# Third layer's heads: the first products and both turns take turns over three PSUM banks, and value products go two key blocks at a time

## The reference

```python
q, k, v = (split_heads(q), split_heads(k), split_heads(v))
scores = jnp.einsum('bhqd,bhkd->bhqk', q, k) * scale
attn = jnp.einsum('bhqk,bhkd->bhqd', jax.nn.softmax(scores, axis=-1), v)
combined = g * mem_out + (1.0 - g) * attn
```

## Time and profile before

| | us |
|---|---|
| median of 3 runs | 4081.96 (4080.65 to 4087.51) |
| profiled execution, its own time | 4091.38 |
| span of the profiled execution | 4089.6 |
| stage of the heads in it | from about 2301 to 2774 |
| TensorE busy over the span | 3655.6 (89%) |
| VectorE busy over the span | 2325.4 (57%) |
| ScalarE busy over the span | 1598.5 (39%) |
| mean granted TensorE clock | 0.929 of full speed |

### The profile page before, as it was taken

One profiled execution on the slowest core, in us unless ns is written; L12 is line 12 of the kernel. 1 busy time (PEld: TensorE's weight loads), 2 busy tenths in 40 slices (PEclk: granted clock), 3 DMA queues, 4 the chain that ended last, 5 costly groups with the idle time before them and its releaser, 6 DMA issues. The chain is left out here.

```text
span 4089.6 us, 65022 instructions
## 1 busy us (share of the span) xinstructions
PE 3655.6 (89%) x21096; PEld 2662.2 (65%) x21096; DVE 2325.4 (57%) x4783; ACT 1598.5 (39%) x2884; POOL 1389.7 (34%) x1087
## 2 busy tenths in 40 slices
PE   6999999999797999999966799997899979999676
PEld 4777777777575888888833344443678737776354
DVE  3555555555325566666647778774566646666444
ACT  2444444444233444444423166662333333333211
POOL 1333333333135666666614000000223352334254
PEclk8999999999898999999978799998899989999755
DMA  0000000000001000000004122210333313332144
GB/s 35 5 5 5 3 5 5 5 3 5 32 0 45 18 17 20 18 17 17 8 3 183 42 74 76 76 65 26 83 82 87 90 34 76 91 82 54 57 103 95
DMA packets 115990, 178.66 MB, mean 44 GB/s; under 512 B 22288, under 2 KB 65040, under 8 KB 115600
## 3 DMA queue, kind: packets, MB, share of 16 engines
q1 hardware_dynamic: 109776, 169.38, 13.8%
q0 software_dynamic: 6144, 8.39, 1.3%
HBM read 151.51 MB, written 25.95 MB: 43 GB/s over the span
## 5 line engine op out<-in xcount | busy, mean ns | idle before, releaser
L424 POOL TENSOR_TENSOR l0h_probs<-l0h_probs,l0h_inv 128x128 f32<-128x128 f32 (+7 forms) x256 | 292.8, 1146 | 585.7 <-DVE l0h_inv L459 585.7
L1747 DVE TENSOR_REDUCE l2h_half<-l2h_s 128x1 f32<-128x512 f32 x512 | 329.6, 685 | 94.2 <-PE l2h_s L1658 94.1
L1734 ACT ACTIVATE l2h_PT<-l2h_s 128x1024 f32<-128x1024 f32 x256 | 261.9, 1023 | 194.2 <-PE l2h_s L1668 194.2
L355 PE MATMUL l0h_sc<-l0a_KT,l0h_QT 128*128 x768 | 296.7, 499 | 30.0 <-ACT l0h_probs L528 28.3
L382 PE MATMUL l0h_cx<-l0h_PT,l0h_VG 128*128 128x128 f32 x2304 | 300.7, 276 | 0.0
L528 ACT ACTIVATE l0h_probs<-l0h_sc,l0h_negtop 128x128 f32<-128x128 f32 (+7 forms) x256 | 189.6, 741 | 245.4 <-DVE l0h_negtop L454 245.0
L382 PEld LDWEIGHTS l0h_cx<-l0h_PT,l0h_VG 128*128 128x128 f32 x2304 | 278.0, 192 | 1.1
L159 POOL TENSOR_TENSOR XN<-XN,n_rstd 128x512 f32<-128x512 f32 x32 | 39.8, 1265 | 635.2 <-DVE n_rstd L140 635.2
L2189 DVE TENSOR_TENSOR_SCAN l3p_table<-l3p_decb,l3p_eye 128x512 f32<-128x512 f32 x128 | 149.8, 1212 | 116.0 <-DMA l3p_prow<-l_decays 92.2
L1658 PE MATMUL l2h_s<-l2h_K,l2h_Q 128*128 128x512 f32 x512 | 180.2, 429 | 21.7 <-DMA l2h_K<-l_split 18.0
L452 DVE TENSOR_REDUCE l0h_top<-l0h_sc 128x1 f32<-128x128 f32 (+7 forms) x256 | 194.0, 758 | 8.8
(11 more groups left out here) (410 smaller groups left out, 9081.1 us busy)
## 6 DMA issues: line engine op xcount, KB each, us to landing
l3p_decb<-l_decays SPq DMA_DIRECT2D x128, 256.0 KB, 5.2
l3p_w<-L_w SPq DMA_DIRECT2D x34, 512.0 KB, 5.9
l2h_Q<-l_split SPq DMA_DIRECT2D x64, 256.0 KB
l2h_K<-l_split SPq DMA_DIRECT2D x64, 256.0 KB
l3p_prow<-l_decays SPq DMA_DIRECT2D x128, 128.0 KB, 5.6
l_split<-l2q_hi SPq DMA_DIRECT2D x16, 512.0 KB, 4.0
l_split<-l2q_lo SPq DMA_DIRECT2D x16, 512.0 KB, 3.8
mx_wgu<-L_ffn_w_gate_up SPq DMA_DIRECT2D x32, 256.0 KB
```

What stands on the lines that cost most here:

```text
L355: mm = pe.matmul(sc[u % 2][:, lo:lo + n], QT[:, u * P:(u + 1) * P], KT[:, ds(g, 1), b * S + lo:b * S + lo + n], start=True, stop=True)
L424: pool.tensor_tensor(p, p, inv[:, u % 4:u % 4 + 1].to_broadcast([P, keys(u)]), ALU.mult).then_inc(probs_scaled, 1)
L1734: act.activation(PT[:, b, kb, :], s2[kb % 2][:, :], ACT.Exp, scale=L2_SCALE).then_inc(exped, 1)
L1747: dve.reduce_max(half[:, b, t, z:z + 1], s1[i % 2][:, :], AX_X).then_inc(maxed, 1)
```

## The change

The first products get three banks instead of two, and the bank of the turns goes: both turns now use the same pool. Each job has 18 slots in a fixed order: products 0 and 1, the maxima's turn (slot 2), the context's turn (slot 3), products 2 to 15 (slots 4 to 17); slot s uses bank s % 3. One semaphore, `s1_read`, counts every read of a slot in this order: the maximum of a product, the second half of the split, the normalisation. Who writes slot s waits until slot s - 3 is read. `read_up_to` works out the count for a slot; the first jobs lack some turns, which it takes into account. `m_ready`, `maxed` and `ctx_kept` go.

TensorE's order changes too. For two key blocks it was S S F F V, S S F F V (S second product, F first product, V the value products of a block). Now it is F S S F S S, then in the first pair of a job the turn of the maxima and the turn of the context, then F F V V. VectorE reads two products, then splits, normalises, and reads the other fourteen (before: four, then twelve). SyncE waits for the split by `s1_read`.

```diff
-        s1 = [st.ps(f"s1_{i}") for i in range(2)]
+        s1 = [st.ps(f"s1_{i}") for i in range(3)]
-        turns, pv = st.ps("turns"), st.ps("pv")
+        pv = st.ps("pv")
-        TURN_AT = 1
+        TOP_SLOT, CTX_SLOT, SLOTS = 2, 3, NP + 2
+        READ_BY_LAST = SLOTS * (L2_N - 2) + 31
+        def slot_of(i):
+            return i if i < TOP_SLOT else i + 2
+        def bank(slot):
+            return s1[slot % 3]
+        def read_ahead(n):
+            if isinstance(n, int) and n < 2:
+                return {-2: 0, -1: NP, 0: 2 * NP + 1, 1: 3 * NP + 2}[n]
+            return SLOTS * n + 31
+        def read_up_to(n, slot):
+            missing = () if not isinstance(n, int) or n >= 2 else (TOP_SLOT, CTX_SLOT) if n == -2 else (CTX_SLOT,)
+            return read_ahead(n) + slot + 1 - sum(m <= slot for m in missing)
...
-                    sp.wait_ge(m_ready, n + 1)
+                    sp.wait_ge(s1_read, top_read(n))
...
-                        wait(pe, maxed, NP * n + i - 1)
-                        pe.matmul(s1[i % 2][:, :], Q1[:, b, t * P:(t + 1) * P], K1[:, b, z * BANK:(z + 1) * BANK],
+                        wait(pe, s1_read, read_up_to(n - 2, slot_of(i) - 3))
+                        pe.matmul(bank(slot_of(i))[:, :], Q1[:, b, t * P:(t + 1) * P], K1[:, b, z * BANK:(z + 1) * BANK],
...
+                def turn_top(n, of, read):
+                    pe.wait_ge(top_ready, n + 1)
+                    pe.wait_ge(s1_read, read)
+                    pe.transpose(bank(TOP_SLOT)[0:NQ, 0:P], top[:, of, :], k.ident[:, :]).then_inc(top_turned, 1)
+                def turn_ctx(j, read):
+                    pe.wait_ge(pv_kept, j + 1)
+                    pe.wait_ge(s1_read, read)
+                    for i in range(2):
+                        mm = pe.transpose(bank(CTX_SLOT)[:, i * P:(i + 1) * P], ctxT[:, i * P:(i + 1) * P], k.ident[:, :])
+                    mm.then_inc(ctx_turned, 1)
...
                 def step(h, b):
-                    for kb in range(NQ):
-                        second_pass(h, b, kb)
+                    n = B * h + b
+                    for kb in range(0, NQ, 2):
+                        for i in range(2):
+                            if exists(h, b, 2):
+                                first_pass(*after(h, b, 2), (2 * kb + i,))
+                            second_pass(h, b, kb + i)
+                        if kb == 0:
+                            if exists(h, b, 1):
+                                turn_top(n + 1, 1 - b, READ_BY_LAST if not exists(h, b, 2) else read_up_to(n, TOP_SLOT - 3))
+                            if not isinstance(h, int) or h > 0:
+                                turn_ctx(n - 2, READ_BY_LAST + 2 * b if not exists(h, b, 2) else read_up_to(n, CTX_SLOT - 3))
                         if exists(h, b, 2):
-                            first_pass(*after(h, b, 2), range(2 * kb, 2 * kb + 2))
-                        if kb == TURN_AT:
-                            turn(B * h + b + 1, not isinstance(h, int) or h > 0, (b + 1) % B if exists(h, b, 1) else None)
+                            first_pass(*after(h, b, 2), (2 * kb + 2, 2 * kb + 3))
                         if not is_first(h, b):
-                            values(*before(h, b), kb)
+                            for i in range(2):
+                                values(*before(h, b), kb + i)
...
-                    early = 2 * (TURN_AT + 1)
                     if more:
-                        maxima(*after(h, b, 2), range(early))
+                        maxima(*after(h, b, 2), range(TOP_SLOT))
```

More of the change, by code:

```diff
@@ L1552, in l2_heads @@
         VH = st.sb("VH", [P, 2, NQ, L2_W])
-        s1 = [st.ps(f"s1_{i}") for i in range(2)]
+        s1 = [st.ps(f"s1_{i}") for i in range(3)]
         s2 = [st.ps(f"s2_{i}", 2 * BANK) for i in range(2)]
-        turns, pv = st.ps("turns"), st.ps("pv")
+        pv = st.ps("pv")
         ctxT = st.sb("ctxT", [P, 2 * P])
-        pmt = turns[0:NQ, NQ * L2_W:NQ * L2_W + P]
         filled, q1_loaded = st.sem("filled"), [st.sem(f"q1_loaded{i}") for i in range(B)]
         q2_loaded, m_loaded = [st.sem(f"q2_loaded{i}") for i in range(B)], [st.sem(f"m_loaded{i}") for i in range(B)]
-        s1_made, maxed, top_ready = st.sem("s1_made"), st.sem("maxed"), st.sem("top_ready")
-        mhi_ready, m_ready, s2_made, exped = st.sem("mhi_ready"), st.sem("m_ready"), st.sem("s2_made"), st.sem("exped")
-        pv_made, pv_kept, turned, inv_ready, ctx_kept = (st.sem(n) for n in ("pv_made", "pv_kept", "turned", "inv_ready", "ctx_kept"))
+        s1_made, s1_read, top_ready = st.sem("s1_made"), st.sem("s1_read"), st.sem("top_ready")
+        mhi_ready, s2_made, exped = st.sem("mhi_ready"), st.sem("s2_made"), st.sem("exped")
+        pv_made, pv_kept, top_turned, ctx_turned, inv_ready = (st.sem(n) for n in ("pv_made", "pv_kept", "top_turned", "ctx_turned", "inv_ready"))
         vh_ready, second_loads = st.sem("vh_ready"), st.sem("second_loads")
         NP = 2 * NQ
-        TURN_AT = 1
+        TOP_SLOT, CTX_SLOT, SLOTS = 2, 3, NP + 2
+        READ_BY_LAST = SLOTS * (L2_N - 2) + 31
         MROW = SPLIT
@@ L1609, in load_second, with top_read @@
                     load(Q2[:, b, :], K2[:, b, :], h, b, q2_loaded[b])
+                def top_read(n):
+                    return READ_BY_LAST + 1 if isinstance(n, int) and n == L2_N - 1 else read_up_to(n - 1, TOP_SLOT)
                 def load_max(h, b):
                     n = B * h + b
-                    sp.wait_ge(m_ready, n + 1)
+                    sp.wait_ge(s1_read, top_read(n))
                     for i, m in enumerate((mhi, mlo)):
@@ L1683, in values @@
                         mm.then_inc(pv_made, 1)
[L1685 to L1690, removed]
-                        for i in range(2):
[L1692 to L1702, removed]
-                    for kb in range(NQ):
-                        second_pass(h, b, kb)
+                def turn_top(n, of, read):
+                    pe.wait_ge(top_ready, n + 1)
+                    pe.wait_ge(s1_read, read)
+                    pe.transpose(bank(TOP_SLOT)[0:NQ, 0:P], top[:, of, :], k.ident[:, :]).then_inc(top_turned, 1)
@@ new lines, in turn_ctx @@
+                def turn_ctx(j, read):
[4 more added lines that the diff above has]
+                    mm.then_inc(ctx_turned, 1)
+                first_pass(0, 0, range(NP))
+                first_pass(0, 1, range(TOP_SLOT))
+                turn_top(0, 0, read_up_to(-1, TOP_SLOT - 3))
@@ new lines, in _, with step @@
+                first_pass(0, 1, range(TOP_SLOT, NP))
+                def step(h, b):
+                    n = B * h + b
+                    for kb in range(0, NQ, 2):
+                        for i in range(2):
+                            if exists(h, b, 2):
[6 more added lines that the diff above has]
+                                turn_ctx(n - 2, READ_BY_LAST + 2 * b if not exists(h, b, 2) else read_up_to(n, CTX_SLOT - 3))
@@ L1712, in _ @@
                 steps(pe, step)
-                turn(L2_N + 1, True, None)
+                turn_ctx(L2_N - 2, READ_BY_LAST + 3)
                 for kb in range(NQ):
                     values(L2_HEADS - 1, B - 1, kb)
-                turn(L2_N + 2, True, None)
+                turn_ctx(L2_N - 1, READ_BY_LAST + 4)
             @block.scalar
@@ L1723, in keep_ctx @@
                     if not is_first(h, b):
-                        act.wait_ge(turned, n + 3)
+                        act.wait_ge(ctx_turned, n)
                     act.activation(ctxT[:, :], pv[:, 0:2 * P], ACT.Copy).then_inc(pv_kept, 1)
@@ L1746, in maxima @@
                         dve.wait_ge(s1_made, NP * n + i + 1)
-                        dve.reduce_max(half[:, b, t, z:z + 1], s1[i % 2][:, :], AX_X).then_inc(maxed, 1)
+                        dve.reduce_max(half[:, b, t, z:z + 1], bank(slot_of(i))[:, :], AX_X).then_inc(s1_read, 1)
                 def take_top(h, b):
                     n = B * h + b
-                    dve.wait_ge(maxed, NP * (n + 1))
+                    dve.wait_ge(s1_read, read_up_to(n - 2, SLOTS - 1))
                     dve.reduce_max(top[:, b, :], half[:, b, :, :], AX_X).then_inc(top_ready, 1)
@@ L1755, in split_max @@
                     n = B * h + b
-                    dve.wait_ge(turned, n + 1)
+                    pmt = bank(TOP_SLOT)[0:NQ, 0:P]
+                    dve.wait_ge(top_turned, n + 1)
                     wait(dve, m_loaded[b], 32 * h)
@@ L1759, in split_max @@
                     dve.wait_ge(mhi_ready, n + 1)
-                    dve.tensor_tensor(mlo[:, b, :], pmt, mhi[:, b, :].bitcast(F32), ALU.subtract).then_inc(m_ready, 1)
+                    dve.tensor_tensor(mlo[:, b, :], pmt, mhi[:, b, :].bitcast(F32), ALU.subtract).then_inc(s1_read, 1)
                 def normalise(h, b):
                     n = B * h + b
-                    out = turns[:, 0:NQ * L2_W].rearrange("p (i g e) -> p g i e", i=2, e=L2_W)
-                    dve.wait_ge(turned, n + 4)
```

(9 more changed lines are left out.)

## The result

The change made the kernel 0.8% faster: 4049.25 us median of 4 runs (4042.39 to 4055.51) against 4082.28 (4080.65 to 4087.51), a ratio of 0.9917 with a 95% interval of 0.9895 to 0.9938. A second set of five runs gave 4052.09 against 4084.99, 0.9916 (0.9903 to 0.9930). The forecast was 4049, or 32.9 us less; the two pairs of medians differ by 33.0 and 32.9. The intervals are some 9 and 6 us either way, so it is luck that the forecast was met to within 0.3 us.

What follows compares the result with a forecast made beforehand. TensorE's own order of work was taken as the bound. 29 jobs x 1.0 us, plus 2.3 at the start and 1.5 at the end, gave 32.9 less than 4082.0: 4049 us, range 4043 to 4056 (chance 0.66).

Steps and rivals of the forecast that it cites:

- The run of value products: TensorE, two blocks' value products in a row: 0.34 us saved per pair (3.06 instead of 3.40), 1.36 a job.
- The stall behind the split: First pair: the fourth first product waits for the split's second half; 0.52 us against 0.18 now, bounds 0.18 and 1.07.
- rival B: Less stall behind the split: 0.18 us, job 12.75, kernel 4039; chance 0.11.
- The waits on counts and the order of SyncE: Added and moved semaphore waits, and SyncE waiting for the split's count: costed at 0; lost cover would cost 0.05 to 0.1 a job.
- The loads: Loads against the next job's second product: slack shrinks by 0.23 us, from 1.6 to 1.4 less the last landing; costed at 0.
- Rival A: Turn's chain (first half: normalisation wait, job 13.65, 4065) or loads without slack (second: 13.33, 4056) take over; chance 0.17.
- The start and the end: First jobs gain 2.3 us (bounds 0 and 4.8), held by job 2's load; last two jobs gain 1.5 (lower bound 0).
- Rival C: TensorE's waits in first pairs bring its clock down to 1.2 GHz: slower, 4123 with a quarter of the stage there; chance 0.03.
- Rival D: No gain: the second block's value rounds do not follow at 0.22 us, the pair stays 3.40, kernel 4088; chance 0.03.

Runs made afterwards that it cites:

- The variant that moves F3: Changed kernel, but in a job's first pair the second late first product stands behind the value products; 4046.55 us, ratio 0.9907 to the kernel before.
- the run with spread loads: Changed kernel with only the loads' rows reordered, 16 features outermost: 4038.49 us; with the late first product also behind the values: 4034.19 us.
- the one with more traffic: Changed kernel with each load of Q1 and K1 made twice, 1.5 MB a job instead of 1: 4147.69 us against 4081.86 before.

## Why the prediction was right

*The run of value products.* Priced at 0.34 us for each of four; 0.35 by the run that puts them back. The pair of 3.06 came out at 3.04 to 3.06. That one number, read from the gaps around one block and from 16 rounds at the end of the stage, carries the result.

*The stall behind the split.* Forecast 0.52, measured 0.60 (V at 2.99 instead of 2.39): VectorE began the split 0.07 later than I had it (1.91 instead of 1.84), and F3's load followed the split's end by 0.06. The variant that moves F3 took back 0.31 of it in the jobs whose loads were in time. Its lower bound, 0.18, and with it rival B, is out; so is the upper bound, since F3's row names the split and not the normalisation.

*The waits on counts and the order of SyncE.* Priced at 0, and no wait but these two stands in TensorE's first pair. A job of 13.13 instead of 13.10 leaves no room for more.

*The loads.* Priced at 0 with 1.4 us less the last landing to spare. The price was right for the changed kernel, by the run with spread loads; the spare time was not. I took the next job's S as the deadline, but the loads issued last, Q1 and K1, are for the first product. It stood 0.58 behind that S and now leads the job 0.34 ahead of it, so their spare time shrank by 0.23 + 0.58 + 0.34 = 1.15 us and not by 0.23. The two waits for a landing in the variant, 0.96 and 0.31 us, stand before this very product. Rival A's second half, that they had no slack, is out for the changed kernel, but came true 0.3 us further down.

*The start and the end.* From the first product to the second pass of job 1 it was 37.5 us and is 35.8: 1.7 saved, forecast 2.3; the load that I named is what held it. (In the second profile of the changed kernel it is 34.8, with a wait of 1.73 for this load instead of 2.45.) From the second pass of job 30 to the end of the stage it went from 26.7 to 24.2: 2.5 saved, forecast 1.5. Between them stand 29 jobs, from 408.5 to 381.0 us: 27.5 saved, forecast 29.1, since a job is 0.03 longer than walked, and job 1, which has no context to turn, saved only 0.3. With 0.4 ahead of the first product that is the 32.1. The steady part was forecast 1.6 too high, the start 0.6 too high and the end 1.0 too low; the sum is better than its parts, by luck.

*Rival C, the clock.* The row says 1.00 over 360 us, with 0.6 us of waiting in every job. The Trainium skill's account of banks in rotation that make the clock swing ("TensorE: Matmul & The Clock Gate", A second HAM failure mode: psum-queue depth-cycling) did not apply here: three banks in rotation kept full clock, as did two banks in the run with paired values, whose loads waited 86.7 us of the 360. In this part of the stage it was lower in one run alone, the one with more traffic (0.92), where jobs lose some 3 us to the loads.

*Rival D* is out by the row of 16 matmuls in 1.07 us.

## What to carry to other kernels

Count the gaps around a change of matmul shape before counting the matmuls: here a run of 32-column products between full-array ones cost 0.34 us beyond its streaming (with the first weight load behind it that nothing covers), a quarter as much as the block's streaming. Longer runs can need more buffers on the other side, as the consumer of the full-array products goes unfed and then gets them in bunches; pairing in the old order, without the third bank, lost 38 us. And in a pool with a fixed order, walk both ways: who waits for the odd users, and for whom they wait.

## What the runs showed of the hardware that I had not expected

The order of a load's rows alone changed how much of the DMA engines it kept busy, and with that its rate. With 4 as the outermost count of a 64-row load it ran at about 100 GB/s with two tenths of the engines' time used; with 16, at 180 to 330 GB/s a slice with mostly nine tenths. The same bytes then took 5 us of a job instead of 11. It isn't free in engine time: over 360 us of the steady part the DMA share went from 0.22 to 0.36, at the same 82 GB/s. I had priced the loads by their bytes and not looked at how their rows were ordered. The Trainium skill has the rule ("DMA: Bandwidth & Descriptors", Rules for kernel authors): the number of engines follows the slowest dimension that isn't 1, so a count of 4 there keeps the transfer to at most four. The trace agrees: in the run with more traffic the share is 0.25 over 360 us, as much as four engines of sixteen busy all the time.
